# Graph attention edge scores: from VectorE products and ScalarE row sums to TensorE transposes and one-column products

## The reference, cut to what matters

```
x1 = x[edges[0]]; x2 = x[edges[1]]                    # 6144 rows of 512 each
e = concatenate([x1, x2], axis=1) @ Ww + bw           # 6144 x 1024
e = e.reshape(-1, 8, 128).transpose(1, 0, 2)          # 8 heads of 128 columns
e = leaky_relu(e, 0.01)
w = (e @ Wa + ba)[..., 0]                             # one score for each edge and head
mat = full((8, 384, 384), -inf).at[:, edges[0], edges[1]].set(w)
mat = softmax(mat)                                    # then mat @ (x @ Wv + bv), ELU, layernorm
```

## Time and profile before

| | us |
|---|---|
| median of 3 runs (lowest, highest) | 927.63 (926.61, 930.39) |
| the profiled execution, its own time | 931.85 |
| its span, first to last instruction | 929.8 |
| TensorE busy, weight loads | 664.9, 336.2 |
| VectorE busy | 544.3 |
| ScalarE busy | 273.2 |
| POOL busy | 231.4 |
| mean granted TensorE clock | 0.825 of full speed |

### The profile page before, as it was taken

The page is one execution under the profiler, slowest core; times in us unless marked ns, Lnnn a source line. Parts: engine busy times, 40 slices in busy tenths (PEclk is TensorE's granted clock), DMA queues, the critical chain, the costliest instruction groups (busy, mean ns, idle before and its releaser), DMA issues.

```text
span 929.8 us, 9900 instructions
## 1 busy us (share of the span) xinstructions
PE 664.9 (72%) x3019; PEld 336.2 (36%) x3053; DVE 544.3 (59%) x1452; ACT 273.2 (29%) x1097; POOL 231.4 (25%) x230
## 2 busy tenths in 40 slices
PE   5942443522317808972779989379999999999997
PEld 2421121201106704441355544234444444444442
DVE  2448986887978995448463242644458544444433
ACT  2105764645651312431131010202222222222222
POOL 4154776776852610000000000011110111111000
PEclk9985555755556958995879999769999999999999
DMA  8597576877749149003000000618999999999970
GB/s 336 206 389 271 161 250 210 248 222 238 231 158 336 57 170 406 35 0 136 1 0 1 0 1 0 233 39 331 399 401 398 392 395 401 396 388 400 387 292 36
DMA packets 46215, 208.04 MB, mean 224 GB/s; under 512 B 8128, under 2 KB 12224, under 8 KB 36560
## 3 DMA queue, kind: packets, MB, share of 16 engines
q1 hardware_dynamic: 26624, 145.43, 40.0%
q0 software_dynamic: 19536, 61.95, 20.3%
HBM read 200.45 MB, written 10.05 MB: 226 GB/s over the span
## 4 chain that ended last, share of the span: by engine, by line
PE 51%; DVE 8%; issue 1%; DMA 1%; ACT 1%; DVEq 0%; POOLq 0%
PE bank L781 13%; PE bank L809 7%; PE bank L801 6%; PE bank L693 4%; PE bank L708 3%; PE bank L514 2%; PE bank L615 2%; PE bank L621 2%; PE bank L770 2%; PE bank L509 2%; PE bank L762 1%; DMA R<-tok_tab,slot_tok 1%; PE bank L726 1%; PE bank L723 1%; DVE sm L1074 1%
## 5 line engine op out<-in xcount | busy, mean ns | idle before, releaser
L558 PE MATMUL bank<-R 128*128 128x384 bf16 x144 | 51.0, 490 | 140.5 <-DVE R L1156 110.7
L892 ACT ACTIVATE R<-R 128x128 f32<-128x128 f32 x384 | 113.3, 296 | 104.0 <-DVE R L1195 85.8
L781 PE MATMUL bank<-R 128*64 128x512 f32 x576 | 133.8, 607 | 0.0
L467 POOL DMA_INDIRECT R<-tok_tab,slot_tok x36 | 36.1, 1002 | 301.9 <-DVE slot_f L1546 301.2
L514 PE MATMUL bank<-R,xT_s 128*128 128x512 f32 x168 | 80.5, 640 | 1.9 <-DMA R<-L_Ww 1.9
L892 ACT ACTIVATION_READ_ACCUMULATOR R<-R 128x1 f32 x384 | 72.1, 188 | 13.7 <-issue 13.5
L558 PEld LDWEIGHTS bank<-R 128*128 128x128 bf16 x144 | 13.5, 120 | 173.2 <-DVE R L1156 129.1
L1558 DVE TENSOR_TENSOR R<-R,bank 128x256 f32<-128x256 f32 x36 | 15.1, 421 | 103.0 <-ACT R L972 103.0
L801 PE MATMUL bank<-R 128*64 128x512 f32 x288 | 73.3, 599 | 0.5 <-ACT R L966 0.5
L809 PE MATMUL bank<-R 128*128 128x512 bf16 x291 | 68.7, 379 | 6.3 <-issue 5.1
L427 POOL DMA_INDIRECT score<-w_e,e_i x48 | 59.4, 1238 | 41.7 <-DVE w_e L1150 29.6
(11 more groups left out here) (327 smaller groups left out, 1132.1 us busy)
## 6 DMA issues: line engine op xcount, KB each, us to landing
R<-L_w SPq DMA_DIRECT2D x72, 1536.0 KB, 10.1
R<-L_w SPq DMA_DIRECT2D x2, 3072.0 KB, 15.0
score<-R POOLq DMA_DIRECT2D x9, 512.0 KB, 14.7
R<-score SPq DMA_DIRECT2D x3, 1536.0 KB, 10.3
R<-L_Ww SPq DMA_DIRECT2D x2, 2048.0 KB, 14.6
R<-L_W SPq DMA_DIRECT2D x4, 1024.0 KB, 9.4
tab_src<-R SPq DMA_DIRECT2D x3, 516.0 KB, 2.7
tab_dst<-R SPq DMA_DIRECT2D x3, 516.0 KB
```

The lines of the kernel that those rows point to most:

```text
L558: last = pe.matmul(pb[s][:, 0:N], oh[:, e % 2, 0, P * s:P * s + P], oh[:, e % 2, 1, :], start=(e == 0), stop=(e == ET - 1))
L781: last = pe.matmul(pb[4 + i % 2][halves[h], :], xeT[i % 2][:, k, halves[h]], w13[(2 * i + h) % NWB][:, k, :], start=(k == 0), stop=(k == K ...
L892: act_.activation(own, own, ACT.Copy, accum_out=w_e3[:, t, h:h + 1]).then_inc(S("heads_summed"), 1)
```

## The change

The product and the eight row sums go. Each half (512 columns) of a summed tile is transposed by four TensorE transposes into one PSUM bank, ScalarE takes it to SBUF with Relu, and for each head TensorE multiplies the transposed 128 x 128 block (as weights) by the single column 0.99 Wa, which gives the 128 sums of that head in one PSUM column. VectorE adds the linear part from PSUM. The banks 3, 4, 5 and 7 serve the transposes in turn, so the keys keep bank 6 alone and come in groups of three tiles. Scores leave two tiles later instead of one. V is projected ahead of the loop; its weights are loaded at the start. The destination rows get tiles of their own (`ab_dst`, which are `ga[9]` to `ga[11]`), so only nine source gathers are issued ahead of the loop and the other four in its first four turns. Two norm rows, wu and wd are loaded when ten tiles have their scores.

```diff
-NGF = 13
+NGS = 13
+NGA = 9
-V_FROM = 4
+KEYS = 3
+Z_BANK = (3, 4, 5, 7)
...
-        prod = [R2[:, 1536:2560], r1(ROW * NGD, 1024)]
+        reluT = [R2[:, 1536:2048], R2[:, 2048:2560], r1(ROW * NGD, 512), r1(ROW * NGD + 512, 512)]
+        ab_dst = ga[NGA:NGA + NT]
+        fill_s = ga[NGS - 1]
...
@@ SP
+            sp.dma_start(wa, a["L0_Wa"].rearrange("(p o) -> p o", o=1)).then_inc(S("rows0_loaded"), 16)
...
+            sp.dma_start(Wv, a["L0_Wv"].rearrange(chunks, p=P)).then_inc(S("Wv_loaded"), 16)
+            sp.dma_start(bvr, a["L0_bv"].partition_broadcast(P)).then_inc(S("Wv_loaded"), 16)
...
-                sp.dma_start(tab_dst[P * t:P * t + P, :], ab[t]).then_inc(S("dst_rows_stored"), 16)
-            sp.dma_start(Wv, a["L0_Wv"].rearrange(chunks, p=P)).then_inc(S("Wv_loaded"), 16)
-            for row, name in ((bvr, "L0_bv"), (g0r, "L0_gamma"), (b0r, "L0_beta")):
-                sp.dma_start(row, a[name].partition_broadcast(P)).then_inc(S("Wv_loaded"), 16)
+                sp.dma_start(tab_dst[P * t:P * t + P, :], ab_dst[t]).then_inc(S("dst_rows_stored"), 16)
+            sp.wait_ge(S("w_ready"), 10)
+            for row, name in ((g0r, "L0_gamma"), (b0r, "L0_beta")):
+                sp.dma_start(row, a[name].partition_broadcast(P)).then_inc(S("bit_w_loaded"), 16)
...
@@ POOL
-                if t >= NGF:
-                    pool.wait_ge(S("rows_added"), t - NGD + 1)
+                if t >= NGS:
+                    pool.wait_ge(S("zT_psum"), 2 * (t - NGS) + 2)
...
-            for t in range(NGF):
+            for t in range(NGA):
                 gather_src(t)
             pool.wait_ge(S("dst_rows_stored"), 16 * NT)
             for t in range(4):
                 gather_dst(t)
             for t in range(ET):
-                if t >= 1:
-                    scatter_score(t - 1)
+                if t >= 2:
+                    scatter_score(t - 2)
                 if t + 4 < ET:
                     gather_dst(t + 4)
-                if NGF <= t + 4 < ET:
+                if t < NGS - NGA:
+                    gather_src(t + NGA)
+                if NGS <= t + 4 < ET:
                     gather_src(t + 4)
...
@@ TensorE
+            pe.wait_ge(S("Wv_loaded"), 32)
+            for t in range(NT):
+                project(t, 3 + t, xT, Wv).then_inc(S("V_psum"), 1)
...
+            def transpose_rows(t):
+                pe.wait_ge(S("rows_added"), t + 1)
+                for half in range(2):
+                    u = 2 * t + half
+                    if t >= 2:
+                        pe.wait_ge(S("edge_relu_ready"), u - 3)
+                        if half:
+                            pe.wait_ge(S("w_ready"), t - 1)
+                    for j in range(4):
+                        o = D * half + P * j
+                        last = pe.transpose(pb[Z_BANK[u % 4]][:, P * j:P * j + P], ga[t % NGS][:, o:o + P], ident[:, :])
+                    last.then_inc(S("zT_psum"), 1)
+            def sum_heads(t):
+                pe.wait_ge(S("edge_relu_ready"), 2 * t + 2)
+                for h in range(H):
+                    last = pe.matmul(pb[Z_BANK[(2 * t + 1) % 4]][:, h:h + 1], reluT[(2 * t + h // 4) % 4][:, P * (h % 4):P * (h % 4) + P], wa,
+                                     start=True, stop=True)
+                last.then_inc(S("sums_psum"), 1)
...
             for e in range(ET):
+                transpose_rows(e)
                 pe.wait_ge(S("onehot_ready"), e + 1)
...
                 last.then_inc(S("onehot_used"), 1)
+                if e % KEYS == 1 and e // KEYS + 1 < ET // KEYS:
+                    edge_keys(e // KEYS + 1)
+                if e:
+                    sum_heads(e - 1)
+            sum_heads(ET - 1)
...
@@ ScalarE
-            for t in range(ET):
-                act_.wait_ge(S("prod_ready"), t + 1)
-                for h in range(H):
-                    own = prod[t % 2][:, P * h:P * h + P]
-                    act_.activation(own, own, ACT.Copy, accum_out=w_e3[:, t, h:h + 1]).then_inc(S("heads_summed"), 1)
+            for u in range(2 * ET):
+                act_.wait_ge(S("zT_psum"), u + 1)
+                if u >= 4:
+                    act_.wait_ge(S("sums_psum"), u // 2 - 1)
+                act_.activation(reluT[u % 4], pb[Z_BANK[u % 4]][:, :], ACT.Relu).then_inc(S("edge_relu_ready"), 1)
...
@@ VectorE
-                dve.wait_ge(S("src_rows_stored"), 16 * NT)
...
+            def store_sums(t):
+                dve.wait_ge(S("sums_psum"), t + 1)
+                tt(w_e3[:, t, :], pb[Z_BANK[(2 * t + 1) % 4]][:, 0:H], ga[t % NGS][:, 2 * D:ROW], ALU.add).then_inc(S("w_ready"), 1)
...
                 tt(ga[j], ga[j], gd[t % NGD], ALU.add).then_inc(S("rows_added"), 1)
-                dve.wait_ge(S("rows_added"), t + 1)
                 if t >= 2:
-                    dve.wait_ge(S("heads_summed"), H * (t - 1))
-                stt(prod[t % 2].rearrange(heads, h=H), ga[j][:, 0:2 * D].rearrange(heads, h=H), 0.0, bc(waR[:, None, :], [P, H, P]),
-                    ALU.max, ALU.mult).then_inc(S("prod_ready"), 1)
-                if t:
-                    add_linear(t - 1)
-            add_linear(ET - 1)
+                    store_sums(t - 2)
+            store_sums(ET - 2)
+            store_sums(ET - 1)
```

More of the change, by code:

```diff
@@ L400, in _ @@
             for q in range(9):
-                pool.dma_start(fill[q], ga[NGF - 1][:, 0:1024]).then_inc(S("score_filled"), 16)
+                pool.dma_start(fill[q], fill_s[:, 0:1024]).then_inc(S("score_filled"), 16)
             pool.wait_ge(S("edge_idx_ready"), 1)
@@ L538, in _ @@
             pe.wait_ge(S("dst_half_ready"), 2 * NT)
-            for e in range(ET):
[L540 to L552, removed]
-                        pe.wait_ge(S("Wv_loaded"), 64)
-                    project(v, 3 + v, xT, Wv).then_inc(S("V_psum"), 1)
+            pe.wait_ge(S("Wv_loaded"), 32)
@@ new lines, in _, with edge_keys @@
+            for t in range(NT):
+                project(t, 3 + t, xT, Wv).then_inc(S("V_psum"), 1)
+            def edge_keys(g):
+                if g:
+                    pe.wait_ge(S("dup_used"), g)
+                for j in range(KEYS + 1):
+                    e = KEYS * g + j - 1
+                    if e < 0:
+                        continue
+                    o = pb[6][:, P * j:P * j + P]
+                    pe.matmul(o, src_h[:, e:e + 1].to_broadcast([P, P]), ident16[:, 0:P], start=True, stop=False)
+                    last = pe.matmul(o, dst_h[:, e:e + 1].to_broadcast([P, P]), ident16[:, P:2 * P], start=False, stop=True)
+                last.then_inc(S("key_psum"), 1)
@@ new lines, in sum_heads @@
+            def sum_heads(t):
[4 more added lines that the diff above has]
+                last.then_inc(S("sums_psum"), 1)
+            edge_keys(0)
+            pe.wait_ge(S("V_ready"), NT)
+            pe.wait_ge(S("wa_ready"), 1)
+            for e in range(ET):
+                transpose_rows(e)
@@ L1157, in _ @@
                 settle()
-                if t % 4 == 0:
-                    g = t // 4
+                if t % KEYS == 0:
+                    g = t // KEYS
                     dve.wait_ge(S("key_psum"), g + 1)
-                    keys = pb[6 + g % 2]
-                    for j in range(4):
+                    for j in range(KEYS):
                         e = t + j
-                        lo = P * (j - 1) if j else 0
-                        go(stt(dup_scr[:, 256 * j:256 * j + P * (j + 1) - lo], keys[:, lo:P * (j + 1)], key_f[:, e:e + 1],
-                               before_s[:, 0:2 * P] if j else tri, ALU.is_equal, ALU.mult, accum_out=dup_f[:, e:e + 1]))
-                    if g:
-                        go(stt(dup_scr[:, P:2 * P], pb[7 - g % 2][:, 3 * P:4 * P], key_f[:, t:t + 1], ones,
-                               ALU.is_equal, ALU.mult, accum_out=dup0_f[:, g:g + 1]))
-                        settle()
-                        go(tt(dup_f[:, t:t + 1], dup_f[:, t:t + 1], dup0_f[:, g:g + 1], ALU.add))
+                        lo = P if e == 0 else 0
+                        go(stt(dup_scr[:, 256 * j + lo:256 * j + 256], pb[6][:, P * j + lo:P * j + 256], key_f[:, e:e + 1],
+                               before_s[:, lo:2 * P], ALU.is_equal, ALU.mult, accum_out=dup_f[:, e:e + 1]))
@@ L1173, in _ @@
                     settle()
[L1174 removed]
+                    stt(row_i[:, t:t + KEYS], dup_f[:, t:t + KEYS], 262144.0, key_f[:, t:t + KEYS], ALU.mult, ALU.add).then_inc(S("dup_used"), 1)
                     dve.wait_ge(S("dup_used"), g + 1)
[L1176 to L1181 removed]
@@ L1190, in _ @@
-                dve.wait_ge(S(f"edge_rows{t % NGD}"), 16 * sum(1 if e < NGF else 2 for e in range(t % NGD, t + 1, NGD)))
+                    dve.wait_ge(S("first_src_rows"), 16 * NGA)
+                if t == NGA:
+                    dve.wait_ge(S("next_src_rows"), 16 * (NGS - NGA))
+                dve.wait_ge(S(f"edge_rows{t % NGD}"), 16 * sum(1 if e < NGS else 2 for e in range(t % NGD, t + 1, NGD)))
```

(1 more changed line is left out.)

53 lines of the change are left out of this document (25 added, 28 removed).

## The result

The changed kernel takes 967.6 us (median of 4, 963.8 to 977.5) against 929.0 for the kernel before (median of 4): ratio 1.041, 95% interval 1.034 to 1.048. It is slower; the forecast was 907, with 922 as the upper end of the range. The rival that came true is the second, TensorE as the bound (958).

The account below looks back on a forecast made before the run. The prediction took POOL's queue, 4.20 us a turn, as the bound. Gains of 7.9 (start), 11.1 (steady part) and 1.3 (tail) sum to 20.3 us, off the median 927.63: 907.3, told as 907, range 897 to 922.

Parts of the forecast that it names:

- The bound: Edge loop: POOL's queue of score writes and gathers sets the pace, 4.20 us a turn, 147 of 158 us.
- TensorE's new work: Edge loop: transposes, head, count and key products take 4.9 us a tile at half clock, 2.9 at full.
- The clock: TensorE in the edge loop: full clock for all but the first tiles, so its work hides behind POOL.
- V ahead of the loop: Ahead of the loop: 12 products, 5.4 us, hidden while first destination rows are fetched; up to 5 without that cover.
- the start: Up to the source gather of tile 13: it goes out at 103.5 instead of 111.36, gain 7.9 us.
- The steady part: Source gather of tile 13 to the last: 34 turns of 4.20, 142.8 us instead of 153.9, gain 11.1.
- rival 1: Edge loop: the stall moves to whichever engine runs many small instructions, POOL keeps its waits; 918.4 us, chance 0.13.
- The waits added: Edge loop: the chain of sum, transposes, Relu and products fits into a turn of 4.2 us; cost 0.
- the loads moved: Loads: one more issue ahead of Ww, +0.5 us; 1.5 MB into the loop, between 0 and 3.7, taken as 0.
- The tail: Last source gather to last score: 9.8 us instead of 11.1, gain 1.3.
- the point of decision: Edge loop: above 4.27 us a tile TensorE becomes the bound.
- Rival 2: Transposes and one-column products of the loop: TensorE stays at half clock and binds, +30 us, 958; chance 0.11.

Follow-up runs that it names:

- a4: The kernel before with only the changed start (loads, V ahead of the loop, own destination tiles), old product and row sums kept: 917.8 us, ratio 0.998.
- d2: The kernel before with only the changed start (loads, V ahead of the loop, own destination tiles), on chip V: 916.1 us, ratio 1.000.
- b3: The changed kernel with four of the eight head products a tile, four heads left out: 934.7 us, ratio 1.002 to the kernel before.
- a1: The changed kernel with each one-column head product widened to 64 equal columns, on chip II: 924.4 us, ratio 1.003 to the kernel before.
- b4: The kernel before with ScalarE's eight row sums of 128 columns replaced by two of 512: 931.8 us, ratio 1.000.
- a2: The changed kernel with rectified rows and the column 0.99 Wa in bfloat16, on chip II: 916.6 us, ratio 0.996 to the kernel before.
- a3: The changed kernel with one of the eight head products a tile, seven heads left out: 920.0 us, ratio 0.999 to the kernel before.
- d3: The changed kernel with each one-column head product widened to 16 equal columns, on chip V: 934.5 us, ratio 1.015 to the kernel before.
- d4: The changed kernel itself, run again on chip V: 943.7 us, ratio 1.027 to the kernel before.
- c4: The changed kernel with head products in bfloat16 and widened to 64 columns, on chip IV: 935.2 us, ratio 1.003 to the kernel before.
- c3: The changed kernel with the same head products split into two runs of four, on chip IV: 983.6 us, ratio 1.055 to the kernel before.
- c2: The changed kernel with each one-column head product widened to 64 equal columns, on chip IV: 954.1 us, ratio 1.022 to the kernel before.

## Why the prediction was wrong, by its steps

**The bound.** "POOL's queue sets the pace", with 4.20 a turn: right for the kernel before. Without waits for the score in the steady part it turned in 4.14 and 4.15 (a4, d2). In the changed kernel POOL's own instructions and pauses made 1.344 + 1.171 + 1.028 + 0.9 = 4.44 us a turn, still within the 0.3 that the prediction allowed; the rest of the 5.28 is its wait for scores.

**TensorE's new work: the step that failed first.** "8 one-column products 4.00 x 8/18 = 1.78" took the x18 of the earlier trace rows for 18 products. They were 9, of two records each: a float32 product is two weight loads and two matmuls. The 24 records of 65 columns were 12 products, so 0.95 at full clock was half too. The term is 3.52 at half clock and 1.90 at full. The row could have been read: the kernel makes 9 such products there, three tiles by three, and the row counts 18. A tile costs 6.58 and 3.51 us, not 4.9 and 2.9, and instead of a budget that mixed levels could meet easily against 4.27, it needs 0.62 of the time at full clock, a granted mean of 0.81 (from 0.62/3.51 + 0.38/6.58 = 1/4.27). Half the records take the loss away at an unchanged clock (b3, to 1.002).

**The clock: the second.** "I take full clock for all but the first tiles" stood on 11 us of transposes and 65-column products. In the loop it alternates; its mean over the turns was 0.66, 0.63 and 0.82 (chips I, III, V). The prediction named pauses as the danger; TensorE was busy for 96 to 97% of the turns, and the clock fell all the same. 64 columns did the most for it (a1 0.97 over the turns, on chip II).

**V ahead of the loop.** The same miscount: 12 products are 24 records, 10.54 us and not 5.4. The first gather came as forecast (63.01; 62.9), the first sum at 71.32 and not 68.2, since V and the keys now stood in front. The sentence on the cover, "if that were gone it would cost up to 5", named the price and dismissed it. The 7.9 us of the start became 0 here and 2.5 (108.83 for 111.36, across chips) in d2, where TensorE is no bound. The late first sum is the smaller part: the first score left at 80.37, 2.3 us after the 78.1 of the forecast, and from there to gather 13 POOL took 30.9 us and not 25.4. Of these 5.5 us 2.8 were its own instructions, of up to 1.98 us, and 2.7 waits for scores.

**The steady part.** 11.1 us were to come from ScalarE's chain. b4 takes the chain away and gains nothing: rival 1 is right that the stall is not ScalarE's own. What was held against it, 228 instructions in 20 us as denser than "the 40 in 4.2", rested on the miscount: with 16 records for the head products a turn has about 59. With TensorE as the bound the turn went to 5.28, 36.7 us from the forecast.

**The waits added, the loads moved.** No cost can be seen: the last store of the destination rows was issued at 59.69 (forecast 60.0), in the turns POOL waited for scores as TensorE was late, and VectorE waited for gathers in the kernels where TensorE was not.

**The tail.** 1.3 us of gain became 5.8 of loss, for the products of five tiles were still to be made when the last gather went out (290.66 to 307.5, 80 records). Behind the loop 3.3 us more remain unexplained; a4 has none of them, and a1, a2, a3, d3 and d4 have 2.8 to 3.6.

**The rivals.** Rival 2 had the place, the point of decision and the sign right, and a price of 30 where the loop cost 31.3; the 4.9, too low, and half clock for the whole time, too much, cancelled. So its 958 beside the measured 967.6 is in part luck. Its budget was too small by a quarter, and it got a chance of 0.11. The prediction and its rival shared the one miscount.

**Open.** What makes instructions come late for "issue" on chips I, III and IV and not on II and V (the page of the kernel before shows 55 packets of instructions fetched by DMA; whether any came late was not tested); and why one-column products go with the low clock on a TensorE that doesn't pause. No kernel that was run is faster than the one before beyond doubt: bfloat16 products had 0.996 on one chip and 1.002 on another.

## What to carry to other kernels

Count TensorE's work in records, not in products: a float32 product is two weight loads and two matmuls here, a float32 transpose one, and a record with one column took as long as its weight load (5.18 us for 45 records and 5.14 for their weight loads at full clock). Eight one-column products cost 1.90 us at full clock and 3.52 at half in float32, and 0.34 to 0.40 in bfloat16. Where a change is to fill an idle engine, price it at the slower clock, and ask for the share of full clock at which it breaks even, before asking how likely that is. A stall whose releaser is "issue" belongs to no engine until an experiment has taken that engine's work away.

## What the runs showed of the hardware

- A one-column float32 product took 0.22 us for each of its two records at half clock (3.52 for 16) and 0.11 at full (3.63 for 32). At full clock 16 records of 64 columns took no longer than 16 of one, so width was free in float32 (a1 first, then the changed kernel). In bfloat16 it was not: eight of 64 columns took 0.41 to 0.64 us (c4), eight of one 0.34 to 0.40.

```profile
179.19 1.89 PE L586 MATMUL bank<-R 128*128 128x64 f32 x16
```

```profile
287.46 1.90 PE L586 MATMUL bank<-R 128*128 128x1 f32 x16
```

- TensorE was busy 167 of 174 us and was granted 0.72 (changed kernel), 171.7 of 174 and 0.57 (c3), but 101.1 of 174 and 0.83 (a3). Being busy by the profile's rows is not what kept the clock. With the head products at 64 columns TensorE was granted 0.96 and 0.85 (a1, c2), busy 153.4 and 149.4 us.
- The "FP8 and Floating Point Precision" page of the Trainium skill (TensorE Precision Notes) speaks of four passes for a float32 product. The records here are two; by time the traces agree with it for wide products: at full clock one of 512 columns took 0.88 us in float32 (10.54 for 12) and 0.24 in bfloat16 (2.12 for 9, L852 of the changed kernel).
